# Gated layer of a decoder kernel: GpSimd keeps its row additions alone, VectorE takes the products and sums, and its order within each step is changed

## The reference

```python
def _L3_attn_ref(x, ...):          # x is layernorm(x) of the stream
    residual = x
    xn = rms_norm(x, g1)
    lin = xn @ W_lin.T + b_lin
    x_gel = gelu(lin)
    x_rg = lin @ W_conv.T + b_conv
    rt = sigmoid(x_rg @ Wa + ba); it = sigmoid(x_rg @ Wx + bx)
    a = exp(-softplus(-Lam) * rt / 8)
    gated = sqrt(1 - a*a) * (it * x_rg)
    h = scan over time of h = a*h + gated      # 256 steps in each sequence
    residual = (x_gel * h) @ W_lin2.T + b_lin2 + residual
    xm = rms_norm(residual, g2)
    gate = gelu(sigmoid(xm @ W1.T + b1))
    y = (gate * (xm @ W2.T + b2)) @ W3.T + b3
    return y + residual
```

## Time and profile before

| | |
|---|---|
| median of 3 runs | 3982.16 us (3981.55 to 3984.32) |
| the profiled execution | 3982.85 us, span of its trace 3981.0 us |
| mean granted clock of TensorE | 0.958 |
| busy TensorE / VectorE / ScalarE / GpSimd | 3627.7 / 3072.0 / 2253.5 / 1427.7 us |
| stretch of the Gated layer, 3460 to 3640 us | TensorE busy 152.83, VectorE 111.59, ScalarE 87.62, GpSimd 40.05 of 180 us |
| its granted clock | 0.94 |

### The profile page before, as it was taken

How to read it: one execution, slowest core, us unless ns; L and a number is a source line. 1 busy time by engine, 2 the same in 40 slices (tenths; PEclk the granted TensorE clock), 3 DMA queues, 4 the chain that set the end, 5 groups by cost and what they waited for, 6 DMA issues and landing times.

```text
span 3981.0 us, 57266 instructions
## 1 busy us (share of the span) xinstructions
PE 3627.7 (91%) x19890; PEld 2550.7 (64%) x19890; DVE 3072.0 (77%) x7103; ACT 2253.5 (57%) x5322; POOL 1427.7 (36%) x928
## 2 busy tenths in 40 slices
PE   6888988999899989999999999788798889989998
PEld 2334334344566768997888897555566568746877
DVE  7999989999787667667888787778577785565777
ACT  7576776776665532223555555578678662254446
POOL 4989888999200000000333234477321200030000
PEclk8998999999999999999999999889999999999999
DMA  4555545657521000000000001000000000100000
GB/s 146 160 152 161 174 150 174 189 182 233 195 86 48 29 25 22 33 12 16 1 1 1 1 1 45 16 1 1 13 2 1 21 25 1 47 0 23 1 1 22
DMA packets 145015, 240.33 MB, mean 60 GB/s; under 512 B 23400, under 2 KB 67696, under 8 KB 142040
## 3 DMA queue, kind: packets, MB, share of 16 engines
q1 hardware_dynamic: 114051, 212.75, 17.2%
q10 hardware_dynamic: 30676, 23.93, 1.8%
HBM read 210.08 MB, written 26.54 MB: 59 GB/s over the span
## 4 chain that ended last, share of the span: by engine, by line
PE 55%; DVE 19%; ACT 5%; issue 4%; POOL 1%; ACTq 0%; DVEq 0%; POOLq 0%
PE PS L209 44%; PE PS L216 8%; DVE db L1315 3%; PE PS L1984 3%; DVE stat L291 1%; DVE p L4004 1%; ACT PS L1280 1%; DVE qg L2481 1%; PE PS L3616 1%; DVE db L1320 1%; DVE p L2495 1%; DVE XNr L328 1%; DVE W L2758 0%; DVE p L3058 0%; POOL far L4146 0%
## 5 line engine op out<-in xcount | busy, mean ns | idle before, releaser
L1315 DVE TENSOR_TENSOR_SCAN db<-PS,db 128x512 f32<-128x512 f32 x512 | 591.7, 1205 | 46.3 <-ACT PS L1280 33.4
L209 PE MATMUL PS<-db,cst 128*128 128x512 f32 x1024 | 500.6, 629 | 26.0 <-DVE db L1320 26.0
L216 PE MATMUL PS<-cst,p 128*128 128x128 f32 (+1 forms) x2880 | 397.9, 284 | 53.5 <-DVE pt L3580 14.7
L2288 POOL TENSOR_TENSOR rb<-rb,tb 128x512 f32<-128x512 f32 x32 | 43.0, 1342 | 1088.7 <-DVE tb L2283 1088.7
L216 PEld LDWEIGHTS PS<-cst,p 128*128 128x128 f32 (+1 forms) x2880 | 332.6, 147 | 128.0 <-issue 61.1
L209 PEld LDWEIGHTS PS<-db,cst 128*128 128x128 f32 x1024 | 202.8, 202 | 289.1 <-issue 237.2
L209 PE MATMUL PS<-xnT,W 128*128 128x256 f32 (+2 forms) x880 | 324.3, 511 | 37.5 <-ACT gate L1112 15.3
L1261 POOL TENSOR_TENSOR db<-W,b 128x1024 f32<-128x1024 f32 x128 | 307.3, 2427 | 59.7 <-DVE W L1197 45.3
L1261 POOL TENSOR_TENSOR db<-du,b 128x1024 f32<-128x1024 f32 x128 | 305.9, 2416 | 37.7 <-PE PS L209 37.0
L209 PEld LDWEIGHTS PS<-xnT,W 128*128 128x128 f32 (+1 forms) x880 | 168.9, 197 | 165.3 <-issue 113.8
L2139 ACT ACTIVATE W<-PS,W 128x512 f32<-128x512 f32 x144 | 98.7, 689 | 288.7 <-PE PS L209 270.9
(11 more groups left out here) (479 smaller groups left out, 8428.4 us busy)
## 6 DMA issues: line engine op xcount, KB each, us to landing
b<-bc_rows SPq DMA_DIRECT2D x256, 256.0 KB, 3.8
c<-bc_rows SPq DMA_DIRECT2D x256, 256.0 KB, 4.0
qk<-fore_qk SPq DMA_DIRECT2D x48, 294.5 KB, 2.9
fore_qk<-W ACTq DMA_DIRECT2D x48, 256.0 KB, 4.3
W<-in_we SPq DMA_DIRECT2D x9, 1024.0 KB, 4.9
W<-in_w SPq DMA_DIRECT2D x50, 128.0 KB, 3.7
fore_v<-W ACTq DMA_DIRECT2D x24, 256.0 KB, 3.2
v<-fore_v SPq DMA_DIRECT2D x6, 1024.0 KB
```

The costliest lines, as they stand in the source:

```text
L209: ins = T.matmul(out, l, r, start=first and i == 0, stop=last and i == len(pairs) - 1)
L216: ins = T.transpose(bank[0:m, c:c + r], s, ident[0:r, 0:r])
L1315: V.tensor_tensor_scan(db[:, f, r], self.ring.PS[:, self.BANKS[x % 3], r], db[:, f, r], 0.0, ALU.mult, ALU.add).then_inc(self.sc.sem, 1)
L2288: e.eng.tensor_tensor(self.rb[t % 2], self.rb[t % 2], self.tb[t % len(self.tb)], ALU.add).then_inc(self.rg.sem, 1)
```

## The change

GpSimd keeps only the eight row additions. They are no longer issued chunk by chunk in phase 8: three (R of c0, X of c0, X of c1) follow the first half of a of c0 in step 2, and five (R of c1, X of c2 and c3, R of c2 and c3) the first half of conv of c1 in step 4 of GpSimd's program. The product of gate and conv output becomes a VectorE operation, `MUL`, at the end of the step of phase 9. The sum of R into X becomes one 128x1024 VectorE operation (`dve_keep`), at the end of the step of phase 15 (c0, c2) or 16 (c1, c3). On VectorE the bias phases 6 and 7, the scan phase 11 and phase 17 now stand in front of the statistics 3 and 13 and the squares 9 within each step.

```diff
-    GEL, SQ = 10, 10.5
+    GEL, SQ, MUL = 10, 10.5, 9.5
     ACT_ORDER = (GEL, 4, 14, SQ, 8, 9, 1)
-    DVE_ORDER = (5, 15, 3, 13, 6, 7, 9, 11, 0, 2, 12, 17, 18)
+    DVE_ORDER = (5, 15, 6, 7, 11, 17, 3, 13, 9, 0, 2, 12, 18, MUL)
+    POOL_ROWS = {0: ((0, "r"), (0, "x"), (1, "x")), 1: ((1, "r"), (2, "x"), (3, "x"), (2, "r"), (3, "r"))}
+    KEEP = (15, 16, 15, 16)
...
-        self.aA, self.qG, self.oD = E.counted("act_p", 4), E.counted("pool_q", 8), E.counted("dve_p", 4)
+        self.aA, self.oD, self.ixD = E.counted("act_p", 4), E.counted("dve_p", 4), E.counted("dve_u", 4)
+        self.rowR, self.rowX = E.counted("pool_q", 4), E.counted("pool_rope", 4)
...
-        self.l2, self.r2, self.xg = E.counted("pe_o", NT), E.counted("dve_osb", NT), E.counted("pool_x", NT)
+        self.l2, self.r2, self.xg = E.counted("pe_o", NT), E.counted("dve_osb", NT), E.counted("dve_lg", 4)
...
         for x in self.DVE_ORDER:
             for c, p in now:
-                if p == x:
-                    self.dve_phase(e, c, p)
+                if p == int(x):
+                    self.dve_phase(e, c, x)
+        for c, p in now:
+            if p == self.KEEP[c]:
+                self.dve_keep(e, c)
...
             for c, p in self.phases(s):
-                buf, R = self.buf[c % 3], self.R[c]
-                if p == 9:
-                    e.wait_ge(*self.iA(2 * c + 2))
-                    e.wait_ge(*self.xcD(2 * c + 2))
-                    G.tensor_tensor(buf[4], buf[4], buf[2], ALU.mult).then_inc(self.qG.sem, 1)
-                elif p == 8:
+                if p == 8 and c in self.POOL_ROWS:
                     e.wait_ge(*self.rowS(2))
-                    e.wait_ge(*self.pm["a"](2 * c + 1))
-                    e.wait_ge(*self.xn(self.order(c, 3)))
-                    for i, a in enumerate((R, X[:, 4 * c:4 * c + 4, :])):
-                        ins = G.tensor_tensor(a, a, self.rows[:, i, :].unsqueeze(1).to_broadcast([P, 4, D]), ALU.add)
-                    ins.then_inc(self.qG.sem, 1)
-                elif p == 12:
-                    e.wait_ge(*self.qG(2 * c + 1))
-                    for j in range(4):
-                        t = 4 * c + j
-                        e.wait_ge(*self.r2(t + 1))
-                        e.wait_ge(*self.x_in(t))
-                        G.tensor_tensor(X[:, t, :], X[:, t, :], R[:, j, :], ALU.add).then_inc(self.xg.sem, 1)
+                    e.wait_ge(*(self.pm["conv"](3) if c else self.pm["a"](1)))
+                    for c2, kind in self.POOL_ROWS[c]:
+                        self.pool_row(e, c2, kind)
+
+    def pool_row(self, e, c, kind):
+        a, i, sig, done = ((self.R[c], 0, self.rowR, self.order(c, 3)) if kind == "r" else
+                           (self.E.X[:, 4 * c:4 * c + 4, :], 1, self.rowX, self.order(c, 0)))
+        e.wait_ge(*self.xn(done))
+        e.eng.tensor_tensor(a, a, self.rows[:, i, :].unsqueeze(1).to_broadcast([P, 4, D]), ALU.add).then_inc(
+            sig.sem, 1)
+
+    def dve_keep(self, e, c):
+        X = self.E.X[:, 4 * c:4 * c + 4, :]
+        e.wait_ge(*self.rowX(c + 1))
+        e.wait_ge(*self.r2(4 * c + 4))
+        for t in range(4 * c, 4 * c + 4):
+            e.wait_ge(*self.x_in(t))
+        e.eng.tensor_tensor(X, X, self.R[c], ALU.add).then_inc(self.xg.sem, 1)
...
         elif p == 11:
             e.wait_ge(*self.sqA(c + 1))
-            e.wait_ge(*self.qG(2 * c + 2))
+            e.wait_ge(*self.ixD(c + 1))
...
+        elif p == self.MUL:
+            e.wait_ge(*self.iA(2 * c + 2))
+            e.wait_ge(*self.xcD(2 * c + 2))
+            V.tensor_tensor(buf[4], buf[4], buf[2], ALU.mult).then_inc(self.ixD.sem, 1)
         elif p == 12:
-            e.wait_ge(*self.qG(2 * c + 1))
+            e.wait_ge(*self.rowR(c + 1))
...
             for t in range(4 * c, 4 * c + 4):
-                e.wait_ge(*self.xg(t + 1))
+                e.wait_ge(*self.xg(c + 1))
                 self.dve_to_x(e, t)
```

More of the change, by code:

```diff
@@ L4636, in pool @@
     def pool(self, e):
-        G, X = e.eng, self.E.X
         self.enter(e)
```

## The result

| kernel | median | lowest to highest | executions |
|---|---|---|---|
| before | 3983.06 us | 3981.55 to 3987.78 | 7 |
| changed | 3963.41 us | 3962.72 to 3978.07 | 7 |

The changed kernel is faster: ratio 0.9954, 95% interval 0.9942 to 0.9967, which is 19.65 us between the medians and 13 to 23 us by the interval. The forecast was 3966.9 us, a gain of 15.3, in a range of 3962 to 3974.

The account below looks back on a forecast made before the run. The Gated layer was taken as bound by VectorE's program order up to 3577 us and by TensorE behind it. 17.7 us gained less two sums of 1.2 gave 15.3; 3982.16 - 15.3 = 3966.9 us, range 3962 to 3974.

Parts of the forecast that it names:

- Step 1: Conv bias pair ahead of the statistics of c2: a of c0 2.13 us earlier, and 1.8 more from full clock.
- step 3: The bias pair of c1 no longer waits for c3's statistics: TensorE's hole of 0.44 us before a of c1 goes.
- GpSimd's rows: Row additions make two 128x4 VectorE operations wait up to 2.0 us each; taken as hidden, 0, with 2.0 for the range.
- Bias of c3: Behind conv of c3 TensorE waits some 0.8 us in place of 3.13; gain up to a of c3 6.7 us.
- VectorE's chain: From the bias of c3 to lin2 of c3: 32.1 us without idle, before 43.1; lin2 starts 17.7 us earlier.
- The waits of 5.7, 1.8 and 0.9 us: VectorE operations lengthened by GpSimd: c0's apply 5.7, a 128x4 operation 1.8, c2's square 0.9 us; all were to go.
- The clock inside the chain: Low clock makes lin2 of c2 take 2.5 us more; costed at 0, covered by the 3.0 us hole before lin2 of c3.
- The two sums behind: Keeps of c1 and c3 delay the turn of c2 and a next-layer turn: paid in full, 1.2 us each.
- The clock in other places: Clock falls on a of c0 (1.8 back) or slows one more product (2.5): 3971.2; chance 0.22, shared with GpSimd's block.
- More than forecast: One of two keeps finds cover, or small operations get in between rows: gain 17.5 us, 3964.7; chance 0.07.
- Held back: VectorE's chain from step 7 stays coupled to TensorE, only the removed waits are won: gain 2.4 us, 3979.8; chance 0.08.
- slower: Clock stays at half from lin2 of c2 on; with eight slow products 9.3 us slower, 3991.5; chance 0.03.

Follow-up runs that it names:

- order_only: The kernel before with only VectorE's new order; products, row additions and sums stay on GpSimd as before: 3975.95 us, ratio 0.9980.
- move_only: The changed kernel with VectorE's old order; products and sums still moved to VectorE, row additions still early: 3982.72 us, ratio 0.9996.
- pool_pad: The changed kernel with eight useless 128x512 GpSimd additions behind the first half of a of c3, nothing waiting for them: 3971.54 us.
- keep_latest: The changed kernel with the sums of R into X of c1 and c3 one step later and that of c0 moved from step 9 to 11: 3964.60 us.
- the keep variants: Four versions of the changed kernel with the sum of R into X of c1, of c3, of both, or of both and c0 later: ratios 0.9948 to 0.9956.
- after_again: The changed kernel run and profiled a second time, no edit: 3965.18 us, ratio 0.9953.
- keep_late: The changed kernel with the sums of R into X of c1 and c3 one step later: 3963.09 us.
- rows_late: The changed kernel with GpSimd's eight row additions back at their old places, two per chunk: 3966.42 us, ratio 0.9955.
- keep_late_again: The changed kernel with the sums of R into X of c1 and c3 one step later, run a second time: 3966.64 us.

## Why the prediction was right, point by point

- **Step 1 and step 3.** Forecast 4.3 us up to conv of c3; measured 4.26: 2.12 by the bias in front of the statistics, the rest by the clock that no longer falls on a of c0 and the vanished 0.44. order_only has the same numbers, so all of it is order.
- **GpSimd's rows are hidden in step 3.** They are, at a waiting of 1.6 and 1.8 us on the two small operations; move_only shows what the same block costs (4.0 us) once a bias stands behind it. I had looked for this cost only under the new order.
- **Bias of c3.** Forecast 6.7 us in sum, measured 6.55; TensorE waits 0.84 us there.
- **VectorE's chain.** Forecast 32.1 us without a gap from the bias of c3; measured from the start of the multiply at 3542.38 to the end of y, 3572.61 + 1.22 = 3573.83, 31.45. Every block had the length of its undisturbed row. Lin2 of c3 is 18.3 us earlier, forecast 17.7. The waits of 5.7, 1.8 and 0.9 us are gone, and pool_pad brings such waits back.
- **Which operations wait.** I wrote that VectorE's SBUF-only operations need what GpSimd holds. That is too wide: statistics read SBUF only and kept 1.39 us (changed kernel) and 1.40 (pool_pad) beside GpSimd. Those that waited are the products, additions and scans (TENSOR_TENSOR and its scan, SCALAR_TENSOR_TENSOR) with both inputs in SBUF, and TENSOR_SCALAR. It changed no term of the sum, as I had lengthened no statistics in it.
- **The clock inside the chain is covered.** It fell (lin2 of c2 6.08 us, forecast 6.25) and cost nothing, but the cover was used up: lin2 of c3 shows no hole, where I had 3.0 minus 2.5. VectorE's y still ends last there (3573.83, lin2 starts at 3573.89), but keep_latest, with 1.2 us less on VectorE, starts lin2 only 0.3 earlier: TensorE is right behind.
- **The two sums behind.** Forecast 1.2 each; the keep variants give 1.15 each.
- **Where the size was off.** Sum forecast 15.3, measured in the layer 16.1 (0.6 of it at the chain). The medians say 19.65. The term that I had put at nothing is the clock in the layers behind: 335.5 to 336.2 us from the third turn to the end in three profiles, against 339.3 in the one of before. TensorE's matmuls, matched one by one, keep the same distances from the third turn on except around the clock's falls. The changed kernel loses 1.6 us at the fall near 120 us behind that turn, regains 3.3 at the next, which before has and no profile of the changed kernel, and the rest comes from falls in the last 110 us. The stretch of 10 us from 184 us behind the turn on, before and then the changed kernel (after_again):

```profile
3821.52:3831.52 10.00, 10.00 (x72) 8.76 (x68) 7.41 (x18) 5.71 (x9) 0.00 (x0) 0.66 0.00 0
```

```profile
3805.70:3815.70 10.00, 9.14 (x85) 7.33 (x86) 6.69 (x17) 7.71 (x13) 0.00 (x0) 1.00 0.00 0
```

  I had allowed some 2 us for it in the range and nothing in the sum. That the median stayed in the range in spite of it, 1.4 us above its lower end, is luck. Its sign isn't something that I could have read from the trace of before: the keep variants, with the same work and 1 to 3 us earlier, get 337.1 to 345.0.
- **The rivals.** The clock in other places came, but as a gain. More than forecast did not come by its mechanism: both sums were paid. Held back and slower did not come: the half clock ended within lin2 of c2, and the 16 matmuls of w1 and w2 of c0 behind it take 7.03 us, full speed.
- **The rule against the change.** The Trainium skill, Perfetto Trace Analysis, section Optimizing Scalar/DVE Operations, says that moving work between VectorE and GpSimd might not help. The total of move_only agrees, 0.4 us, though its chain did win 8.3; the whole change, 16.1 us in the layer, does not: after the move nothing of GpSimd's is beside the chain.

## What to carry to other kernels

Work on GpSimd isn't free because nobody waits for it: look in VectorE's timeline for operations longer than their undisturbed likes and for a GpSimd instruction that ends with them, and place GpSimd's blocks where VectorE reads PSUM or takes statistics, or where nothing hurries. In an in-order step put what the next engine waits for first and the statistics last; a step's order and the place of the other engine's work have to be tried together, since each half alone gave 10.95 and 0.44 of 16.14 us. Judge a change of 0.1% by distances between landmarks inside the trace, not by the total.

## What the hardware showed that I had not expected

- One 128x4 VectorE operation can wait for four GpSimd instructions in a row (10.64 us), where in the thirteen other profiles it waited for at most one (1.4 to 2.0 us) at the same place. It explains 9.2 us of the one execution of 3978.07 us. It does not explain every slow one: the profiled 3974.76 us of keep_late has 1.41 us there.
- GpSimd waits for VectorE too: row additions of 3.13 and 2.98 us in place of 2.0 (rows_late), a product of 3.33 in place of 2.34 (order_only).
- One fall of the clock behind the layer repeats with the kernel: keep_late, keep_late_again and keep_latest all show it 29.5 to 29.8 us behind the third turn, and order_only at 28.8, while the ten other profiles have none there. Later falls do not all repeat: keep_late has one from 190.0 to 196.8 us, keep_late_again none there. Why a shift of 1 us in the layer decides the first is open; it wasn't tried separately.
